# PV products of 64 columns on pairs of sequences and head halves, with V's rows from columns that are kept twice

## The reference

```python
def reference(x, ids, lang, cond_w, wq, wk, wv, wo, W, Wr, A, B, up, down, perm):   # x: 32 sequences x 32 tokens x 512
    c = einsum('bct,bcd->bdt', x, cond_w[ids])          # a 32x32 matrix for each sequence mixes its tokens
    q, k, v = (heads(c @ w.T) for w in (wq, wk, wv))    # 32 heads of 16
    q, k = rope(q), rope(k)
    attn = softmax(where(causal, q @ k.T / sqrt(16), -inf))     # 32 x 32 for each sequence and head
    x = x + (attn @ v) @ wo.T
    base = x @ W.T
    gates = top-2 softmax of (x @ Wr.T + 5 * onehot(lang))      # 8 experts
    z = base + 2 * sum over experts of gates * ((x @ A.T) @ B.T)
    return x + unpermute(down @ gelu(up @ z[:, perm]))          # in 16 blocks of 32 columns
```

## Time and profile before

| | |
|---|---|
| Median of 3 runs | 211.14 us (210.86 to 211.37) |
| Profiled execution | 212.6 us, its span 210.8 us |
| TensorE busy | 203.4 us, 2520 matmul instructions |
| VectorE, ScalarE, GpSimd busy | 145.8, 122.4, 116.3 us |
| Granted TensorE clock, mean | 0.992 |

### The profile page before, as it was taken

The page is one execution under the profiler, slowest core; times in us unless marked ns, Lnnn a source line. Parts: engine busy times, 40 slices in busy tenths (PEclk is TensorE's granted clock), DMA queues, the critical chain, the costliest instruction groups (busy, mean ns, idle before and its releaser), DMA issues.

```text
span 210.8 us, 5957 instructions
## 1 busy us (share of the span) xinstructions
PE 203.4 (96%) x2520; PEld 176.6 (84%) x2520; DVE 145.8 (69%) x284; ACT 122.4 (58%) x215; POOL 116.3 (55%) x92
## 2 busy tenths in 40 slices
PE   7999999999989999999999999999999999798993
PEld 5999887998769899987779899986698987788863
DVE  2697999999738877846827797646778994258123
ACT  2587475288843336289944444399865777434460
POOL 4255999598950201978985013969988253524000
PEclk9999999999988999999999999999999999999999
DMA  6999603023010230000044410000045100224002
GB/s 198 387 399 371 214 3 104 0 65 138 0 53 3 100 103 0 3 2 5 0 53 53 145 58 0 3 0 3 4 51 129 23 5 3 25 28 50 0 3 100
DMA packets 9930, 15.18 MB, mean 72 GB/s; under 512 B 1328, under 2 KB 5680, under 8 KB 9904
## 3 DMA queue, kind: packets, MB, share of 16 engines
q1 hardware_dynamic: 7712, 11.89, 16.6%
q0 software_dynamic: 2048, 2.88, 8.3%
q10 hardware_dynamic: 144, 0.02, 0.1%
HBM read 11.13 MB, written 3.67 MB: 70 GB/s over the span
## 4 chain that ended last, share of the span: by engine, by line
PE 89%; ACT 4%; DVE 3%; DMA 1%; issue 1%; ACTq 0%
PE ps_A L625 11%; PE ps_F L625 10%; PE ps_A L627 10%; PE ps_A L626 10%; PE ps_F L626 9%; PE ps_F L627 9%; PE ps_S L778 5%; PE ps_F L868 5%; PE ps_S L756 3%; PE ps_S L883 3%; PE ps_A L681 2%; PE ps_A L778 1%; PE ps_A L896 1%; DMA y<-in_ids 1%; ACT pbd L1056 1%
## 5 line engine op out<-in xcount | busy, mean ns | idle before, releaser
L572 POOL TENSOR_TENSOR pr<-pr,small 128x512 f32<-128x512 f32 x16 | 17.5, 1108 | 39.3 <-DVE small L1422 39.1
L1056 ACT ACTIVATE pbd<-pr 32x512 f32<-32x512 f32 x56 | 35.2, 629 | 1.3 <-DVE pr L1428 0.6
L552 POOL DMA_INDIRECT out<-y,row_at x12 | 19.8, 1646 | 11.3 <-ACT y L1056 8.8
L1118 ACT ACTIVATE pr<-pr 128x512 f32<-128x512 f32 x16 | 10.1, 633 | 23.1 <-DVE pr L1414 23.1
L1162 ACT ACTIVATE act<-ps_F 128x512 f32<-128x512 f32 x32 | 16.5, 604 | 11.3 <-PE ps_F L868 11.3
L509 POOL TENSOR_TENSOR rot<-rot,cst 128x512 f32<-128x512 f32 x11 | 14.3, 1303 | 15.2 <-DVE rot L1380 15.2
L1400 DVE TENSOR_TENSOR kbd<-kr,cst 128x512 f32<-128x512 f32 x13 | 19.0, 1491 | 3.0 <-POOL kr L513 3.0
L522 POOL TENSOR_TENSOR kbd<-kr,cst 128x512 f32<-128x512 f32 x15 | 19.3, 1319 | 0.1
L625 PE MATMUL ps_F<-x,w2T 128*128 128x256 f32 x56 | 16.1, 287 | 0.0
L626 PE MATMUL ps_F<-x,w2T 128*128 128x256 f32 x56 | 15.6, 279 | 0.0
L627 PE MATMUL ps_F<-x,w2T 128*128 128x256 f32 x56 | 15.6, 279 | 0.0
(11 more groups left out here) (238 smaller groups left out, 655.3 us busy)
## 6 DMA issues: line engine op xcount, KB each, us to landing
xs<-in_x SPq DMA_DIRECT2D x4, 512.0 KB, 5.9
xt<-in_xT SPq DMA_DIRECT2D x4, 512.0 KB, 4.5
out<-xt SPq DMA_DIRECT2D x3, 512.0 KB, 3.0
act<-in_L_attn_wk SPq DMA_DIRECT2D x1, 1024.0 KB, 7.4
act<-in_L_attn_wv SPq DMA_DIRECT2D x1, 1024.0 KB, 9.3
act<-in_L_attn_wo SPq DMA_DIRECT2D x1, 1024.0 KB, 7.5
pr<-in_L_attn_wq SPq DMA_DIRECT2D x2, 256.0 KB, 4.2
pr<-in_L_attn_wq SPq DMA_DIRECT2D x1, 512.0 KB, 5.3
```

The lines of the kernel that those rows point to most:

```text
L552: pool.indirect_dma_start(out=out, out_offset=bass.IndirectOffsetOnAxis(ap=row_at[:, g, c:c + 1], axis=0), in_=y[:, c, :], in_offset=None, ...
L572: pool.tensor_tensor(pr[:, i, :, :], pr[:, i, :, :], mx[:, i, :].unsqueeze(2).to_broadcast([P, NH // 2, T]), ALU.mult).then_inc(normed, 1)
L1056: return sc.activation(dst, src, ACT.Copy)
```

## The change

- PV: the rows of a probability block are now (head half, one of 2 sequences, 32 keys) instead of 4 sequences. A product has 64 columns (2 sequences) instead of 128, no two add up, and a chunk still has 8. `wo`'s rows are reordered on the host to the heads' new places.
- Scores write bank s for the pair of sequences s, in the strip 2 * (half) + q; `half_at` gives the row half its place, so both row halves of a pair of products now write to the same bank, in different strips.
- The probabilities are copied on all 128 partitions, twice, each time scaled by the mask `pair`; what had to be zero comes from the mask, so the zeroing of `pbd`, `kbd` and `vz` goes away.
- V: the stationary is 128 columns of `xc` beginning at 0 or 64, and gives one half of the heads each, so 24 products of 256 columns. For this `xc` has 192 columns a tile: the first 64 are kept again behind the 128. `cond_hi` and `cond_lo` write half 0 to both places (`twice`); in group 0 GpSimd copies it (`first_again`), and V waits for that. `v_out` is three scaled copies: one of 128 x 512, two of 128 x 256.
- One idle product more at the start, and in group 0 `v_out(1, 1)` stands ahead of `k_blocks(1, 0, 0)` on ScalarE.

```diff
@@ buffers
-        xc = sb("xc", [P, 2, KC, N], F32R)
+        xc = sb("xc", [P, 2, KC, GT, 3 * P // 2], F32R)
-        vz = sb("vz", [P, 3, NH // 2, 3 * HD])
+        vz = sb("vz", [P, 3, NH // 2, 4, HD])
-        pbd = sb("pbd", [P, 2, NH // 2, BT, T])
+        pbd = sb("pbd", [P, 2, NH // 2, 2 * T])
@@ GpSimd
-            pool.memset(vz[:, 0:2, :, :], 0.0).then_inc(vz_zero, 1)
+            def first_again():
+                for h in range(2):
+                    wait_read(pool, first_cond(h, 0))
+                for part in range(2):
+                    pool.tensor_copy(half_of(part, 2), half_of(part, 0)).then_inc(xc_again, 1)
-                for b in range(2, BT):
-                    at = slice(T * b, T * b + T)
-                    pool.tensor_copy(pbd_of(G - 1, 1, i)[at, :, b, :], pT(2 + i)[at, :, :]).then_inc(pbd_p, 1)
+                pool.tensor_scalar(pbd_of(G - 1, 1, i)[:, :, T:2 * T], pT(2 + i), con("pair")[:, 1:2], None, ALU.mult
+                                   ).then_inc(pbd_p, 1)
-            pool.memset(pbd[:, 1, 0:HC, :, :], 0.0).then_inc(pbd_zero, 1)
             perm_rows()
+            first_again()
-                if g == 0:
-                    third_v()
-                    kbd_zeros(0)
-                    kbd_zeros(1)
@@ TensorE: v
+                if (g, t) == (0, 0):
+                    pe.wait_ge(xc_again, 2)
-                    last = mm3(bank(it)[:, :], xc[:, 0, k, P * t:P * t + P], xc[:, 1, k, P * t:P * t + P],
-                               W[:, 0, k, :], W[:, 1, k, :], k == 0, k == KC - 1)
+                    for r in range(2):
+                        at, half = slice(P // 2 * r, P // 2 * r + P), slice(D // 2 * r, D // 2 * r + D // 2)
+                        last = mm3(bank(it)[:, half], xc[:, 0, k, t, at], xc[:, 1, k, t, at],
+                                   W[:, 0, k, half], W[:, 1, k, half], r == 0 and k == 0, r == 1 and k == KC - 1,
+                                   skip=True)
@@ TensorE: scores
+                        s, q = divmod(b, 2)
-                            last = pe.matmul(bank(its[r])[T * b:T * b + T, P * c:P * c + P],
+                            strip = T * (2 * half_at(s, r) + q)
+                            last = pe.matmul(bank(its[s])[strip:strip + T, P * c:P * c + P],
@@ TensorE: pv
-                for e in range(2):
+                s = c // 2
+                for k in (2 * (c % 2), 2 * (c % 2) + 1):
+                    at = P * k + P // 2 * s
                     for j in range(4):
-                        last = pe.matmul(bank(it)[32 * j:32 * j + 32, P * c:P * c + P],
-                                         vz_of(g, t)[:, 4 * c + j, HD * e:HD * e + 2 * HD],
-                                         pbd_of(g, t, c // 2)[:, HC * (c % 2) + 2 * j + e, :, :],
-                                         start=(e == 0), stop=(e == 1), skip_group_check=True)
+                        last = pe.matmul(bank(it)[32 * j:32 * j + 32, at:at + P // 2],
+                                         vz_of(g, t)[:, 4 * k + j, 2 * s:2 * s + 2, :],
+                                         pbd_of(g, t, s)[:, 4 * k + j, :], start=True, stop=True,
+                                         skip_group_check=True)
-            idle_products(5, rings["S"][0])
+            idle_products(6, rings["S"][0])
@@ ScalarE
-                sc.activation(half_of(0, r), by_half(it), ACT.Copy).then_inc(xc_hi, 1)
+                if r == 0:
+                    sc.activation(twice(0), over_tiles(bank(it)[:, :], P // 2), ACT.Copy).then_inc(xc_hi, 1)
+                else:
+                    sc.activation(half_of(0, r), by_half(it), ACT.Copy).then_inc(xc_hi, 1)
-                copy(dst, bank(it)[:, :].rearrange("p (q s f) -> p q s f", s=2, f=HD)).then_inc(s_free(it), 1)
+                heads = bank(it)[:, :].rearrange("p (r q f) -> p q r f", r=2, f=HD)
+                sc.activation(vz_of(g, t)[:, :, 0:4:3, :], heads, ACT.Copy, scale=con("half")[:, 0:1])
+                for r in range(2):
+                    last = sc.activation(vz_of(g, t)[:, :, 2 - r, :], heads[:, :, r, :], ACT.Copy,
+                                         scale=con("half")[:, 1:2])
+                last.then_inc(s_free(it), 1)
-                for b in range(BT):
-                    at = slice(T * b, T * b + T)
-                    last = copy(pbd_of(g, t, i)[at, :, b, :], pT(2 * t + i)[at, :, :])
+                for q in range(2):
+                    last = sc.activation(pbd_of(g, t, i)[:, :, T * q:T * q + T], pT(2 * t + i), ACT.Copy,
+                                         scale=con("pair")[:, q:q + 1])
-            for i, h in ((0, 0), (0, 1), (0, 2), (0, 3), (1, 2), (1, 3)):
-                copy(pbd[:, i, HC // 2 * h:HC // 2 * h + HC // 2, :, :].rearrange("p h b t -> p (h b t)"),
-                     vz[:, 0, :, :].rearrange("p a b -> p (a b)")[:, 0:HC // 2 * P]).then_inc(pbd_zero, 1)
+                    v_out(1, 1)
                     k_blocks(1, 0, 0)
-                    v_out(1, 1)
@@ VectorE: cond_lo
+                if r == 0:
+                    hi = half_of(0, r).rearrange("p c t n -> p (c t) n").bitcast(F32)
+                    ve.tensor_tensor(twice(1), over_tiles(bank(it)[:, :], P // 2),
+                                     hi.unsqueeze(2).to_broadcast([P, GT * KC, 2, P // 2]), ALU.subtract
+                                     ).then_inc(s_free(it), 1)
```

More of the change, by code:

```diff
@@ L49 @@
 for _name, _n in [("select", SC * T), ("pair", 2), ("pos", 1), ("expert", E), ("ident", P), ("cos", T), ("sin", T),
-                  ("causal", T), ("head", HG), ("pick", E), ("tie", E * E)]:
+                  ("causal", T), ("head", HG), ("half", 2), ("pick", E), ("tie", E * E)]:
     _AT[_name] = (_W, _W + _n)
@@ L74, in constants @@
     put("head", (p // HD % HG)[:, None] == np.arange(HG)[None])
+    put("half", (p // (2 * T))[:, None] == np.arange(2)[None])
     put("pair", (p // T % 2)[:, None] == np.arange(2)[None])
@@ L155, in ropes_to @@
             return 4 * g + i if g else min(i + 1, 3)
-        kbd_pbd = [kbd[:, i, :, :, :].rearrange("p c b k -> p (c b k)").rearrange("p (h b t) -> p h b t", b=BT, t=T)
-                   for i in range(2)]
+        kbd_pbd = [kbd[:, i, :, :, :].rearrange("p c b k -> p (c b k)")[:, 0:NH // 2 * 2 * T].rearrange(
+            "p (q k) -> p q k", k=2 * T) for i in range(2)]
         def pbd_of(g, t, i):
-            return kbd_pbd[i] if (g, t) == (G - 1, 1) else pbd[:, i, :, :, :]
+            return kbd_pbd[i] if (g, t) == (G - 1, 1) else pbd[:, i, :, :]
         def pT(i):
@@ L1105, in v_out @@
                 it = A(g, V + t)
-                if g < 2 and t == 0:
-                    sc.wait_ge(vz_zero, g + 1)
-                    if g == 0:
-                        sc.wait_ge(pbd_zero, 7)
+                if (g, t) == (0, 0):
+                    sc.wait_ge(d_con, 16)
+                if (g, t) == (1, 0):
+                    wait_full(sc, prep("w2", KC - 1))
                 if GT * g + t >= 3:
@@ L1432, in probs_half @@
                 ve.wait_ge(turned, 4 * (G - 1) + i + 3)
-                ve.wait_ge(kbd_zero, i + 1)
-                for b in range(2):
-                    at = slice(T * b, T * b + T)
-                    last = ve.tensor_copy(pbd_of(G - 1, 1, i)[at, :, b, :], pT(2 + i)[at, :, :])
-                last.then_inc(pbd_v, 1)
+                wait_full(ve, S_scores(G - 1, 2 * i + 1))
+                ve.tensor_scalar(pbd_of(G - 1, 1, i)[:, :, 0:T], pT(2 + i), con("pair")[:, 0:1], None, ALU.mult
+                                 ).then_inc(pbd_v, 1)
             def o_lo(g, t):
-                at = slice(P * t, P * t + P)
-                o = attn
-                split_lo(PVi(g, t), o[:, 0, :, at], o[:, 1, :, at], o_hi, GT * g + t + 1)
+                split_lo(PVi(g, t), attn[:, 0, :, t, :], attn[:, 1, :, t, :], o_hi, GT * g + t + 1)
             def add_x(g, i):
@@ L1724, in laid_out @@
         a[n] = a[n][heads].T
-    for n in ("L0_attn_wv", "L0_attn_wo"):
-        a[n] = a[n].T
+    a["L0_attn_wv"] = a["L0_attn_wv"].T
+    pairs = np.array([(16 * r + 4 * c + j) * HD + d for c in range(KC) for j in range(4) for r in range(2)
+                      for d in range(HD)])
+    a["L0_attn_wo"] = a["L0_attn_wo"].T[pairs]
     a["L0_cond2_Wr"] = np.pad(a["L0_cond2_Wr"].T, ((0, 0), (0, T - E)))
```

59 lines of the change are left out of this document (28 added, 31 removed).

## The result

The changed kernel takes 210.59 us (median of 14; 208.35 to 214.11), the kernel before in the same comparison 211.26. The ratio is 0.9944, interval 0.9919 to 0.9970 (the ratios leave out executions far above the fastest of their kernel). It is faster by 0.6% where 2% was forecast, and lies above the range. The profiled execution took 213.41 us, span 211.6.

A forecast was written before the change was run, and what follows sets the result against it. TensorE was taken as the bound (busy 203.4 of 210.8 us). Start +0.1, start and group 0 -0.4, router +0.4, groups 1 and 2 -3.4, group 3 -0.8 sum to -4.1: 211.14 to 207.0 us, range 206.2 to 208.0.

The forecast's parts named there:

- PV at 0.58 a block (0.59 forecast): PV blocks of half a tile: halved columns save 0.42 us of 1.01 each, leaving about 0.59.
- V's products and scores at 0: V's 24 products of 256 columns cost the same as 12 of 512, and scores are unchanged: 0 each.
- rivals 3 and 4: 3: PV blocks save nothing worth naming, 211.5 us, chance 0.10. 4: scores sharing a bank run slower, 214.6 us, chance 0.07.
- Groups 1 and 2: All eight PV blocks in these groups count with 0.42 us each: -3.4 us.
- the routers: Groups 0 and 1: the doubled cond copy ahead of the x1 remainder makes it 0.2 us late, twice: +0.4 us.
- start and group 0 together bring -0.4: Up to group 1's mask product, at 60.45 instead of 60.87 us: -0.4 us, the wider cond copy's 0.6 included.
- GpSimd's two copies: Start, group 0: these copies of 512 elements fit where GpSimd sat idle and cost 0.
- The wide cond: First cond copy of group 1 writes 1024 elements, one half doubled on VectorE: +0.6 us at 33.63.
- the full 1.3 us of three shorter PV blocks: Group 0: three PV blocks ahead of the second V block's end bring that end 3 x 0.42 us earlier.
- Group 3: First tile's PV saves 2 x 0.42 us, -0.8; the second tile gives 0, since TensorE waits for ScalarE there.
- Rival 1: Clock: the 1.2 GHz stretch from 61.3 to 64.8 us, costing 1.7 us, goes away: 205.3 us, chance 0.21.
- Rival 2: More waits: V's copy in three pieces or a second low clock stretch holds TensorE 1.5 us more: 208.5 us, chance 0.19.

The follow-up runs named there:

- `a_nocopy`: Changed kernel without GpSimd's two copies in group 0, that third place in `xc` cleared at the start instead: 210.39 us, ratio 0.9962.
- `b_pv_v`: Kernel before with PV products of 64 columns (half of PV left out) and V as 24 products of 256 columns: 208.86 us, ratio 0.9860.
- the repeat: The changed kernel measured once more with nothing altered: 210.18 us, ratio 0.9931.
- `b_pv_half`: Kernel before with PV products of 64 columns (two of four sequences left out), nothing else changed: 208.48 us, ratio 0.9789.
- `c_last_open`: Changed kernel, cond written once, GpSimd copying in every group, last tile's masked copies on VectorE, idle products in gaps except before that PV: 207.26 us, ratio 0.9796.

## Why the prediction was right or wrong

**Right.** PV at 0.58 a block (0.59 forecast), V's products and scores at 0: rivals 3 and 4 fell. (Rival 3's terms add up to 211.7, not 211.5.) A PV instruction comes every (0.58 - 0.14) / 32 = 14 ns on average, with its load over 128 rows. The Trainium skill's floor of some 25 ns ("TensorE: Matmul & The Clock Gate", Back-to-back issue gap) isn't there, nor does a bank shared by two row halves cost anything, against Gotcha 1 of its page "TensorEngine Tiling (Array Packing)". V's copy in front of the K block saves 0.3. Groups 1 and 2: -3.4 and +0.4 for the routers were forecast, about -3.1 was measured (-1.8 from 61.98 to group 2's scores, with the 1.7 us added that its extra low stretch costs, and -1.3 behind them).

**The first step that failed: "start and group 0 together bring -0.4".** It was +1.1 (61.98 against 60.87), 1.5 off. I looked for TensorE's and ScalarE's queues there. But VectorE runs without a gap from the landed weights (13.23) to the end of K's last rope step (54.88), and TensorE waits 0.54 for that step ahead of the second V block. Before, TensorE came there 0.7 after VectorE was done (the rope step ends at 53.52, the PV block ahead of V at 54.26):

```profile
52.85 0.67 DVE L1382 TENSOR_TENSOR kr<-ps_A,cst 128x512 f32<-128x512 f32 x1
...
53.18 1.08 PE L778 MATMUL ps_S<-pbd,vz 128*32 128x128 f32 x32
```

So V's second block ends at 57.9, where the prediction had 56.5; that is 1.4 of the 1.5. The first three of these things make it up, and the fourth adds to it:
- "GpSimd's two copies ... fit between its gathers and 18.09 ...: 0". GpSimd had the time, VectorE beside it did not: 0.7 (`a_nocopy`). That the two lock each other out of a shared pair of SBUF ports is in the Trainium skill ("SBUF — State Buffer", SBUF: two separate sides); the trace agrees, since the cast of 0.17 took 0.59 and ended at 16.10, when half of the two copies' 1.43 was over.
- The wide cond, +0.6, was right. But the sum set the full 1.3 us of three shorter PV blocks against it. VectorE gains almost nothing from shorter PV: from the mask product of tile (0,1) to that rope step it takes 19.7 us in after (35.19 to 54.88) and 19.9 before (33.63 to 53.52). TensorE had 0.7 us to gain until it meets VectorE there, and every delay of VectorE's row comes off that. Where the row isn't lengthened, 1.1 of the 1.3 is there (`b_pv_v`).
- The weights landed late in this execution; see below.
- V's copy takes 0.69 + 0.83, 1.41 from start to end in a run, not 1.15.

How much of the 1.1 is the change's own? ScalarE's first copy of wk, which waits for the landing, starts at 12.13 here and at 11.10 in the profile of before. From it to the mask product of tile (0,1) it takes 23.1 us here and in the repeat (11.79 to 34.84), and 21.8 in `b_pv_half` and `b_pv_v` (11.42 to 33.23, 11.67 to 33.47). The 1.3 between them are the 0.7 and the 0.6. Three other profiles with full PV have that copy at 11.5 to 11.7 and group 1's mask product at 61.1 to 61.2. An estimate from these: with a landing like theirs, 0.5 earlier, the changed kernel's would be at 61.5, 0.3 to 0.4 late instead of 1.1.

**Group 3, "-0.8".** -0.5. GpSimd's masked copy of 128 x 512 takes 1.67 us a piece, the two of 32 partitions it replaces 1.44, and it is what PV and then the second gelu wait for. 0.3 (`c_last_open`). I had costed ScalarE's copies and passed over this one.

**The second step that failed: the clock.** The sum at full clock, +1.1 - 3.1 - 0.5 = -2.5, is also what the spans show, but both have one execution behind them; with the estimate above the sum would be about -3.2. From there to the -0.7 of the medians it is the clock, 1.8 us, more than any other term. Rival 1 had this backwards. The sum took the low stretch of the one profiled execution as common to all, and let only a rival change it. In fact most executions of before have none (69 of 97), the median one of after has two, and these cost some 2 us (206.5 to about 208.7). Rival 2 ("a second low stretch of the clock") named the mechanism and gave it 1.5, but on top of a sum that was already too good.

**What stays open.** That filling the gaps keeps the clock up is shown: with them filled, 33 of 36 executions of five versions of the changed kernel are at full clock, unfilled 3 of 68 of six. But `b_pv_half` and `b_pv_v` have gaps of 1.5 as well and are at full clock in 6 of 12. Which difference brings low stretches from half of the executions to nearly all (waits of 2.0 and 1.9 for 1.5 and 1.5 are a guess) was not isolated. The landing of the weights, 11.1 to 12.1 us over the profiles, was seen in one execution of each kernel only.

## What to carry to other kernels

Before a gain on the busiest engine is summed up stretch by stretch, look for the engine that has no gap in that stretch (here VectorE up to 55 us): the gain ends where the busiest engine has to wait for it, and whatever slows it, even a neighbour's copy through shared ports, is paid once that point is reached. Take the clock from all executions, not from the profiled one. When a matmul gets shorter, new gaps can bring stretches at the lower level (3.4 or 6.8 us long here); cheap products in the gaps kept the clock up, and were worth 1.0 to 1.7 us of the median here.
